# Perceiver layer with a routed expert stage: one wait less before a copy, and another set of weight parts multiplied whole

## What is computed

```python
probs = jax.nn.softmax(logits, axis=-1)
route_p = jnp.max(probs, axis=-1)
route_idx = jnp.argmax(probs, axis=-1)
h = jnp.einsum('nd,edm->enm', x_flat, W1) + b1[:, None, :]
h = jax.nn.relu(h)
y = jnp.einsum('enm,emd->end', h, W2) + b2[:, None, :]
out = y[route_idx, jnp.arange(n)] * route_p[:, None]
```

## Time and profile before

| what | value |
|---|---|
| median of three runs | 472.65 us (471.93 to 472.70) |
| the profiled execution, its time | 477.21 us |
| its span, first to last instruction | 475.4 us |
| mean granted TensorE clock | 0.953 |
| TensorE busy | 422.6 us, 89% of the span |
| VectorE busy | 322.9 us, 68% |
| ScalarE busy | 250.2 us, 53% |
| nine windows of the expert stage | from 214.38 us to about 457 us of the span |

### The profile page before, as it was taken

How to read it: one execution, slowest core, us unless ns; L and a number is a source line. 1 busy time by engine, 2 the same in 40 slices (tenths; PEclk the granted TensorE clock), 3 DMA queues, 4 the chain that set the end, 5 groups by cost and what they waited for, 6 DMA issues and landing times.

```text
span 475.4 us, 5476 instructions
## 1 busy us (share of the span) xinstructions
PE 422.6 (89%) x1620; PEld 293.9 (62%) x1620; DVE 322.9 (68%) x506; ACT 250.2 (53%) x379; POOL 36.2 (8%) x41
## 2 busy tenths in 40 slices
PE   0999999989999899479999899999999999999940
PEld 0846657547999345457677475767667575767620
DVE  2786869873222198557787797879797896969712
ACT  4787869623000002136577575757667675857610
POOL 2100000000000001000020100202020010202023
PEclk9997999988999999588999999999999999999985
DMA  7995362980002990010006999769797998700005
GB/s 251 418 415 212 123 231 63 345 299 0 0 1 65 408 389 23 6 44 3 0 24 227 360 384 395 266 246 355 301 364 296 355 377 320 263 1 22 1 22 176
DMA packets 33694, 95.71 MB, mean 201 GB/s; under 512 B 2690, under 2 KB 3330, under 8 KB 32132
## 3 DMA queue, kind: packets, MB, share of 16 engines
q1 hardware_dynamic: 30900, 91.61, 51.6%
q0 software_dynamic: 1136, 3.67, 2.3%
q10 hardware_dynamic: 1632, 0.11, 0.2%
HBM read 91.72 MB, written 3.67 MB: 201 GB/s over the span
## 4 chain that ended last, share of the span: by engine, by line
PE 82%; DVE 6%; ACT 4%; DMA 3%; issue 3%; POOL 1%; DVEq 1%; SPq 0%; POOLq 0%; ACTq 0%
PE bank L1414 44%; PE bank L1266 7%; PE bank L1254 6%; PE bank L1235 5%; PE bank L1429 4%; PE bank L1302 2%; DMA ring<-in_wq_t 2%; PE bank L1188 2%; PE bank L1309 2%; PE bank L1243 2%; PE bank L1278 1%; DVE work L1079 1%; DVE w_lo L1098 1%; ACT ring L505 1%; DMA work<-y_rows,icols 1%
## 5 line engine op out<-in xcount | busy, mean ns | idle before, releaser
L1098 DVE TENSOR_TENSOR w_lo<-ring,w_hi 128x1024 fp32r<-128x1024 f32 x108 | 135.1, 1295 | 9.2 <-ACT w_hi L665 9.2
L665 ACT ACTIVATE w_hi<-ring 128x1024 fp32r<-128x1024 f32 x108 | 112.8, 1055 | 35.6 <-PE bank L1414 35.0
L1414 PE MATMUL bank<-ring,work 128*128 128x512 f32 x144 | 67.8, 603 | 0.0
L1414 PE MATMUL bank<-w_hi,x_hi 128*128 128x512 f32 x144 | 49.0, 422 | 5.0 <-DVE w_lo L1098 5.0
L1414 PE MATMUL bank<-w_hi,x_lo 128*128 128x512 f32 x144 | 45.3, 396 | 0.0
L1414 PE MATMUL bank<-w_lo,x_hi 128*128 128x512 f32 x144 | 45.2, 396 | 0.0
L1414 PEld LDWEIGHTS bank<-ring,work 128*128 128x128 f32 x144 | 25.8, 189 | 25.7 <-issue 23.3
L690 ACT ACTIVATE h_hi<-work 128x512 fp32r<-128x512 f32 x36 | 22.7, 631 | 26.5 <-DVE work L1085 25.9
L1166 POOL TENSOR_TENSOR small<-small,work 128x512 f32<-128x512 f32 x9 | 17.2, 1912 | 241.1 <-ACT small L671 241.1
L1414 PEld LDWEIGHTS bank<-w_hi,x_hi 128*128 128x128 f32 x144 | 26.6, 191 | 14.5 <-DVE w_lo L1098 7.9
L1266 PE MATMUL bank<-ring 128*128 128x128 f32 x128 | 35.0, 454 | 0.0
(11 more groups left out here) (184 smaller groups left out, 611.3 us busy)
## 6 DMA issues: line engine op xcount, KB each, us to landing
ring<-in_w SPq DMA_DIRECT2D x32, 2048.0 KB, 9.8
ring<-in_ctx_turned SPq DMA_DIRECT2D x4, 2048.0 KB, 12.0
ring<-in_ctx SPq DMA_DIRECT2D x4, 2048.0 KB, 14.7
y_rows<-small POOLq DMA_DIRECT2D x9, 256.0 KB, 5.3
work<-in_b SPq DMA_DIRECT2D x8, 256.0 KB, 5.4
ring<-in_wq_t SPq DMA_DIRECT2D x1, 1024.0 KB, 9.3
x_sb<-in_x SPq DMA_DIRECT2D x1, 1024.0 KB, 11.7
out<-x_sb SPq DMA_DIRECT2D x4, 256.0 KB, 2.9
```

Source lines behind the costliest of these rows:

```text
L665: act.activation(w_hi[:, n % NSPLIT, :, :], weight_part(e, n), ACT.Identity).then_inc(hi_ready, 1)
L1098: dve.tensor_tensor(w_lo[:, n % NSPLIT, :, :], weight_part(e, n), w_hi[:, n % NSPLIT, :, :], ALU.subtract).then_inc(lo_ready, 1)
L1414: ins = pe.matmul(dst, kept, moved, start=start and g == 0 and q == 0, stop=stop and g == 1 and q == len(terms) - 1)
```

## The change

It has four pieces.

- `WHOLE` becomes (6, 14, 15). Parts 12 and 13 (o2) are split now, part 14 is whole, so both parts of o3 are whole. A window has 13 split parts instead of 12.
- `block_may_copy` waits for the output product before only where one of its parts is whole, since only a whole part reads `hid`. For the copy of block 3 that product is o1, parts 10 and 11, both split, so this wait goes. (The copy of block 0 loses its wait for o2 of the window before in the same way.)
- Block 3 has no halves any more: `block_high(w, 3)` and `block_low(w, 3)` are gone. o3 waits for `h_relu[1]` instead of `h_lo_ready[1]`, and the counts of `h_hi_ready[1]` and `h_lo_ready[1]` are one a window.
- `split_high` and `low_part` of 14 go, those of 12 and 13 come. On VectorE they stand between the copy of block 3 and the low half of block 2, on ScalarE between the copy of block 2 and its relu.

```diff
-WHOLE = (6, 12, 13, 15)
+WHOLE = (6, 14, 15)
...
         def block_may_copy(eng, p, w, k):
             wait_block(eng, w, "h", 2 * k + p)
-            eng.wait_ge(h_lo_ready[p], 2 * w + k + 1)
-
-            wait_block(eng, w, "o", 2 * k + p - 2)
+            if p == 0 or k == 1:
+
+                eng.wait_ge(h_lo_ready[p], 2 * w + k + 1 if p == 0 else w + 2)
+
+            before = 2 * k + p - 2
+            if not {2 * BLOCKS.index(("o", before % 4)) + g for g in range(2)}.isdisjoint(WHOLE):
+                wait_block(eng, w, "o", before)
...
-                wait_block(act, w, "o", i - 2)
+                wait_block(act, w, "o", i - 2 if p == 0 else i - 4)
...
                         block_copy(w, 1)
+                        for n in range(12, 14):
+                            split_high(e, w, n)
                         block_relu(e, w, 1)
                         block_high(w, 2)
-                        for n in (14,):
-                            split_high(e, w, n)
-                        block_high(w, 3)
...
-                dve.wait_ge(h_hi_ready[p], 2 * w + k + 1)
+                dve.wait_ge(h_hi_ready[p], 2 * w + k + 1 if p == 0 else w + 1)
...
                         block_copy(w, 1)
+                        for n in range(12, 14):
+                            low_part(e, w, n)
                         block_low(w, 2)
                         block_relu(e, w, 1)
-                        low_part(e, w, 14)
-                        block_low(w, 3)
...
-                pe.wait_ge(h_lo_ready[p], 2 * w + k + 2)
+                if i == 3:
+                    pe.wait_ge(h_relu[p], 2 * w + k + 2)
+                else:
+                    pe.wait_ge(h_lo_ready[p], 2 * w + k + 2 if p == 0 else w + 2)
```

## The result

The changed kernel takes 460.62 us (median of 4 runs, 460.28 to 463.20) against 472.67 us of the kernel before (4 runs). The ratio is 0.9729 with a 95% interval of 0.9674 to 0.9785, so it is faster. The forecast was 460.5 us, and the range 458.0 to 465.0 holds it.

A forecast was written before the change was run, and what follows sets the result against it. TensorE's own sequence and its gaps were taken to bound the kernel. 0.94 + 0.61 - 0.36 = 1.19 us a window, nine windows 10.7, plus 1.5: 12.2 off 472.65 gives 460.5 us, range 458.0 to 465.0.

The forecast's parts named there:

- The wait: At turn 3: without the wait for o1, block 3's copy starts earlier and turn 3 follows o1, gaining 0.94 us a window.
- TensorE's work: From turn 3 to the window's end: one whole part less and a cheaper switch shorten TensorE's sequence by 0.61 us a window.
- The switch: Transposes followed by a whole part instead of a split one: claimed to cost TensorE 0.38 us more.
- The new wait: At o2: the low half of block 2 queues behind those of parts 12 and 13, costing 0.36 us a window.
- The second and third window: VectorE's list ends earlier, so 1.5 us of these two windows' 1.8 us excess was to go, once.
- B: At o2: VectorE and ScalarE hand over faster, so no new wait; 457.2 us, chance 0.06.
- C: At o2: a gap as long as the removed one, only TensorE's own work gains; 465.7 to 467.2 us, chance 0.12.
- D: Low halves of parts 12 and 13 stretched by GpSimd's bias addition, o2 waits 2.2 us longer; 480.5 us, chance 0.02.
- E: Block 3's copy still comes after o1, each window 1.9 us longer; some 488 us, chance 0.02.

The follow-up runs named there:

- the reordered version: Changed kernel with VectorE's low half of block 2 between those of parts 12 and 13, ScalarE's split of part 13 after block 2's high half: 456.75 us.

## Why the prediction was right, and where it was not

**The wait, 0.94 us a window.** Right as far as it went: turn 3 follows o1, and the copy starts 0.29 us behind h3, where I had 0.32. But the same removal also took the wait for the low half of block 2 that stood behind the late copy. With only this edit a window gains 1.20.

**TensorE's work, 0.61 a window.** This is the step that was mis-sized: "That leaves 7.24 - 1.38 - 3 x 1.71 = 0.73 for the transposes ahead of a whole part: that switch costs 0.38 more." The switch costs 0.10, by the pair of runs with part 12 split and whole (25.07 and 25.40, of which 0.23 is the part itself). The other 0.26 was a wait for `h_lo`, which the difference of starts cannot tell from work, since copy, turn 3 and low half always stood at the same distances. The new parts gain 0.33 a window.

**The new wait, 0.36.** Measured 0.42: the low half of block 2 began 3.16 us behind h3's end, where I had 3.18, and o2 followed it by 0.82 us, where I took 0.74 from the copy and turn 3.

**The second and third window, 1.5.** Measured 1.8, all that there was. The reason given, that VectorE's list ends earlier, is borne out by the run with part 12 whole against the run with only the wait removed: equal ordinary windows, 0 against 2.0 us.

The sum closes: 0.94 + 0.26 + 0.33 - 0.42 = 1.11 us a window, which is 26.60 - 25.49; nine of them and 1.8 are 11.8, against 11.9 measured. The total of 12.2 was right because the 0.38 was booked under the wrong name but in the same place: the removed wait and the new parts both take it away, so the mistake did not show. The rest are small errors, 0.08 a window too much and 0.3 too little in the third, which offset each other in part. That the median then fell within 0.1 us of the forecast is luck, with executions that differ by 3 us. Under its right name the judgement on the change differs: the new set of parts does not pay in an ordinary window (0.33 gained, 0.42 given back; 25.49 against 25.40 with the wait alone). It pays at the start of the third window, where VectorE's list became shorter at its end.

**The rivals.** B, no new wait, is what the reordered version reaches, at 25.07. C did not happen; the gap at which it would leave no difference is 0.94 + 0.61 = 1.55 us by its own terms, not 1.4. D's mechanism exists and costs nothing where it stands in the changed kernel. E, the copy still behind o1, was tried as an experiment: its windows of 28.5 were right, but its price of 488 left out the clock, and 498.9 was measured.

The six matmuls of part 13 take 1.36 us in the profile after (282.97 to 284.33) and 1.38 before, so the trace differs from the estimate, and the rows were the right choice.

## What to carry to other kernels

When a wait sits ahead of a queue of instructions, its price is not only the gap it shows: look at who waits for each instruction behind it, since a constant distance between two starts may be a second wait that hides as duration. The list of weight loads may name it where the list of matmuls does not. After such a wait is gone, the next limit is the order within the queue; here moving one instruction in each of two lists, at no cost in work, was worth 0.42 us a window, more than the 0.33 of the new parts. And what a list ends with matters at the loop's odd passes, where the engine has its longest pause.

## What was not expected of the hardware

A gap of TensorE of about 0.94 us ahead of turn 3 and one of about 2.6 us ahead of o2, with four transposes between them, brought the granted clock to half, 1.2 GHz, for some 3.4 us in seven of nine windows. There the stall cost its own length and another 1.6 us. A single gap of 1.56 us (the low half of part 13 done twice) left the clock at 1.00 in all eight windows behind the first. Whether the gap of 2.6 us alone would do it is not shown.

The pause of TensorE inside part 1 of the third window, between two matmuls that no semaphore separates, took 0.3 to 1.2 us beyond the usual distance in the three profiles with the early low half and part 12 split, and did not occur in the other profiles of the changed kernel and its variants.

A VectorE subtraction of 1.2 us took up to 2.1 us beside GpSimd's addition of 1.8 us, and never did with the addition cut to 8 columns. The stretch itself was seen before; that the addition causes it is what the run adds.
